# A decoder layer with attention, retention and routed experts on one core: first stage reordered, norm factor on ACT, transposes that accumulate

## The chip, the cores and the metric

The program runs on one core of a Trainium2 chip. Its time is device microseconds: the median of three runs is 1015.34 us (1014.36 to 1017.56).

## The reference

x and ctx have 128 sequences of 64 tokens of 128 dimensions, float32. Three blocks follow each other, each with its residual and a layer norm without weights.

```python
def layernorm(x): return (x - mean(x)) / sqrt(var(x) + 1e-5)

def reference(x, ctx, Wq, Wk, Wv, Wo, bo, gate, w1, w2, w3):
    # 1. self-attention, 16 heads of 8
    q, k, v = (heads(t @ W.T) for t, W in ((x, Wq), (x, Wk), (x, Wv)))
    att = softmax(q @ k.T / sqrt(8))
    x = layernorm(x + merge(att @ v) @ Wo.T + bo)
    # 2. retention: scores with a decay mask, no softmax
    q, k, v = xpos(heads(x)), xpos(heads(ctx), downscale=True), heads(ctx)
    x = layernorm(x + merge((q @ k.T * decay) @ v))
    # 3. two of eight experts per token, inner size 512
    w, e = top_k(x @ gate, 2); w = softmax(w)
    y = sum(w[i] * ((silu(x @ w1[e[i]]) * (x @ w3[e[i]])) @ w2[e[i]]) for i in (0, 1))
    return layernorm(x + y)
```

The shape in the first block is unusual: `x` has 128 sequences, and attention runs among the 64 tokens of each.

## The kernel before

It has three stages. The **first stage** takes 32 pairs of tiles (a tile is 128 tokens, two sequences) through both attention blocks, computes the gate, and scatters each token's row twice (once for each chosen expert) to DRAM (`xs`, "routed_rows"). The **second stage** gathers 71 tiles of 256 routed rows of one expert each, runs the expert, and scatters the results to "token_halves". The **third stage** adds the two halves of a token and norms.

All engines run the first stage in lockstep of a kind, without a common clock. `run_steps` (L178) writes out, for each engine, its steps in a row; in step s a function that stands at `at(lag)` works on item s - lag. Since `A_FIRST` is 32, all of the first stage is written out, without a loop. The order of an engine's work is the order of the `at` calls in its own `step` function, by hand: L457 on SyncE, L715 on PE, L975 on ACT, L1331 on DVE, L1571 on POOL. Each function first waits on semaphores (`wait`, `wait_ring`, `wait_last`) and counts up one of its own. Where PSUM is shared between engines, `wait_last` (L150) names, of several events, the one that comes last in that order.

An item's way: SyncE loads x (L461). PE transposes it (`tokens_across`, L532), ACT copies it to `x_t` (L858), PE projects q, k, v (L540), ACT copies q and v (L865). DVE forms all products of q and k (`products`, L1145), PE sums them over dimensions (`scores`, L556), DVE and PE find the maximum over all keys (L1155 to L1174, L567 to L577), DVE subtracts it, ACT takes the exponential (L873). POOL multiplies by v (`weighted`, L1545, eight instructions), PE sums over keys (`sums`, L579), DVE divides (L1182, L1189). SyncE stores the heads to DRAM, waits for that store, and reloads them in transposed order (L468 to L481). PE adds projection, bias and x (`residual`, L593). Then the first norm: DVE has statistics (`spread`, `moments`), then `variances` (L1224) for the first norm of one item and the second norm of an earlier one together (`NORM_GAP` = 2), POOL raises to the power -0.5 and forms the shift (L1523, L1534), ACT applies them (`first_norm`, L898). PE transposes keys and queries, as sums of two products with the identity (L610, L619). Retention scores, mask, values and head selection follow (L639, L1235, L649, L663), the second residual and norm (L1242, L944), the gate and the top two with their ranks (L675 to L703, L1252 to L1329), and POOL's indirect scatters (`scatter`, L1559). ACT's second norm writes into a ring of four, so it waits for the scatters of the item four before it (L948).

Three weight matrices are loaded in float32 and split into a high and a low half-precision part during the first steps, on DVE and ACT (L1108 to L1143, L835); their loads stand at the head of ACT's queue (L829). `stand` (L404) writes a marker and counts a semaphore; it occurs in all three stages.

The lines that the prediction's steps touch:

```python
wait_ring(it, routed_out, RING, 64)                    # second_norm, L948
wait(it, marked[n], 1)                                 # stand, L407
wait(it, nb_ready)                                     # first_norm, L901
eng.matmul(XKT[:, P * u:P * u + P], xk_a[:, u, :], ident, start=True, stop=False)   # keys_across, L615
```

## Time and profile before

| | |
|---|---|
| median of 3 runs | 1015.34 us |
| profiled execution, its span from first to last instruction | 1027.0 us |
| PE busy | 839.8 us (82%), 12164 instructions |
| DVE busy | 794.7 us (77%), 2219 |
| POOL busy | 654.8 us (64%), 738 |
| ACT busy | 607.7 us (59%), 1416 |
| DMA | 72.7 MB, mean 71 GB/s |

The time of the profiled execution is known by its span alone; it is 1.1% above the median of the timed runs. In the profile, PE is the matrix engine and PEld its weight loads, DVE the vector engine, ACT the scalar engine, POOL the general one and SP the engine that only issues transfers. A row of a group of instructions gives the line, engine, operation, what is written and read with its shape, how many; then the busy time in us and the mean duration of one in ns; then the idle time of the engine just before them and what ended it. The means of one instruction hold its whole way through the engine, so instructions that follow each other overlap. A granted clock of 1.00 is 2.4 GHz on PE, 0.50 is 1.2 GHz, and a number in between is a mix over the stretch.

### The profile page before, as it was taken

Reading aid. Unit: us, or ns where it says so; the run is one execution under the profiler, and the core shown is the slowest. Engines: PE = TensorE matmul, PEld = TensorE weight load, DVE = VectorE, ACT = ScalarE, POOL = GpSimd, SP = SyncE. Lnnn points to the kernel's source line nnn. Section 1 sums busy time; section 2 is a strip of 40 time slices with the busy share of each in tenths; the row PEclk is TensorE's granted clock in tenths of the full one; section 3 lists DMA queues with packets and bytes.
Section 4 is the critical chain, followed back from the end, with each engine's and each line's share of the span. In section 5 each row is a group of like instructions: output and inputs, shape, how many; then the busy total and the mean of one; then the engine's idle time right before and its main releaser. Section 6 shows DMA issues by size and latency. Waiting matters only on the chain.

```text
span 1027.0 us, 35115 instructions
## 1 busy us (share of the span) xinstructions
PE 839.8 (82%) x12164; PEld 639.6 (62%) x12164; DVE 794.7 (77%) x2219; ACT 607.7 (59%) x1416; POOL 654.8 (64%) x738
## 2 busy tenths in 40 slices
PE   1667699999999999989979770699999999999600
PEld 1445466666666666656655440599899999999500
DVE  4787899998988989878856642588888888888575
ACT  1123457667667777666766851466666666666355
POOL 0338776699989999988997456044444444444443
PEclk9687899999999999999998965799999999999855
DMA  9312122122232231212222002222222222222186
GB/s 307 79 27 48 35 52 54 36 66 67 47 72 52 65 68 50 65 37 60 47 50 63 23 22 63 66 64 61 61 63 65 65 62 64 63 61 59 45 257 222
DMA packets 145303, 72.72 MB, mean 71 GB/s; under 512 B 75024, under 2 KB 134544, under 8 KB 145136
## 3 DMA queue, kind: packets, MB, share of 16 engines
q1 hardware_dynamic: 124800, 40.56, 17.1%
q0 software_dynamic: 8640, 17.84, 5.2%
q10 hardware_dynamic: 11696, 12.08, 3.6%
q8 instruction: 105, 1.72, 0.7%
q14 instruction: 62, 0.51, 0.2%
HBM read 42.11 MB, written 28.34 MB: 69 GB/s over the span
## 4 chain that ended last, share of the span: by engine, by line
PE 33%; POOL 28%; issue 11%; DVE 3%; DMA 2%; another core or an unknown queue 1%; ACT 1%; POOLq 0%; SPq 0%; DVEq 0%; ACTq 0%
POOL prod_ev L1551 14%; POOL routed_rows L1568 9%; PE QKV L773 9%; PE ST L773 9%; PE XT L801 5%; PE SC L801 5%; POOL rs L1531 3%; DMA prod_ev<-token_halves 1%; DMA routed_rows<-xe,pos 1%; PE YY L589 1%; POOL frs L1613 1%; PE YY L791 1%; PE TR L791 1%; PE SC L562 1%
## 5 line engine op out<-in xcount | busy, mean ns | idle before, releaser
L1551 POOL TENSOR_TENSOR prod_ev<-e_sb,q_v 128x512 f32<-128x512 f32 x256 | 300.3, 1206 | 77.5 <-PE YY L589 40.1
L1600 POOL DMA_INDIRECT token_halves<-w_new,tok_i x142 | 137.9, 971 | 32.5 <-issue 22.2
L1568 POOL DMA_INDIRECT routed_rows<-xe,pos x128 | 131.2, 1025 | 30.4 <-issue 30.0
L1151 DVE TENSOR_TENSOR prod_qk<-q_v,QKV 128x2048 f32<-128x2048 f32 x64 | 145.4, 2274 | 4.9 <-ACT q_v L870 4.9
L1453 DVE TENSOR_TENSOR prod_ev<-prod_qk,prod_ev 128x1024 f16<-128x1024 f32 x71 | 87.0, 1225 | 56.1 <-ACT prod_ev L1028 31.1
L773 PE MATMUL QKV<-k_t,w_hl 128*128 128x256 f16 x852 | 117.2, 274 | 0.0
L773 PE MATMUL ST<-k_t,w_hl 128*128 128x256 f16 x852 | 116.9, 274 | 0.0
L411 POOL TENSOR_TENSOR marks<-half_c 128x1 f32<-128x1 f32 x103 | 19.7, 192 | 149.7 <-DVE w_new L1469 149.1
L1037 ACT ACTIVATE prod_qk<-QKV,silu_scale 128x512 f32<-128x512 f32 x142 | 90.0, 683 | 41.3 <-PE QKV L773 41.3
L1028 ACT CAST prod_ev<-prod_qk 128x1024 f16<-128x1024 f32 x71 | 74.2, 1045 | 62.9 <-DVE prod_qk L1479 62.9
L1479 DVE SCALAR_TENSOR_TENSOR prod_qk<-ST,hid_scale,prod_qk 128x512 f32<-128x512 f32 x142 | 99.5, 742 | 2.9 <-PE ST L773 1.8
L924 ACT ACTIVATE q<-XT,tab 128x256 f32<-128x256 f32 x256 | 96.6, 495 | 0.0
L589 PE MATMUL YY<-prod_ev,tab 128*32 128x144 f32 x2048 | 83.3, 304 | 11.4 <-DVE m_two L1167 7.2
L951 ACT ACTIVATE xe<-res,nb,rs 128x128 f32<-128x128 f32 x128 | 52.7, 483 | 64.3 <-DMA routed_rows<-xe,pos 64.3
L773 PEld LDWEIGHTS ST<-k_t,w_hl 128*128 x852 | 83.7, 98 | 10.0
L1239 DVE TENSOR_TENSOR sm<-ST,tab 128x1024 f32<-128x1024 f32 x64 | 77.7, 1215 | 15.2 <-PE ST L643 12.9
L773 PEld LDWEIGHTS QKV<-k_t,w_hl 128*128 x852 | 80.9, 98 | 9.0 <-issue 0.4
L643 PE MATMUL ST<-q,k_t 64*64 64x512 f32 x512 | 74.2, 651 | 8.1 <-ACT q L924 5.4
L589 PEld LDWEIGHTS YY<-prod_ev,tab 128*32 128x32 f32 x2048 | 62.3, 115 | 24.7 <-issue 23.2
L562 PE MATMUL SC<-prod_qk,tab 128*32 128x256 f32 x1024 | 68.0, 408 | 10.7 <-ACT e_sb L878 6.8
L1531 POOL TENSOR_TENSOR rs<-ve,half_c 128x4 f32<-128x4 f32 x34 | 37.8, 1113 | 45.6 <-DVE ve L1233 44.4
L801 PE MATMUL XT<-w_hl,prod_ev 128*128 x864 | 61.2, 223 | 3.1 <-DVE prod_ev L1453 3.1
(171 smaller groups left out, 1785.9 us busy)
## 6 DMA issues: line engine op xcount, KB each, us to landing
w_new<-routed_rows SPq DMA_DIRECT2D x71, 130.0 KB
prod_ev<-token_halves SPq DMA_DIRECT2D x16, 512.0 KB, 4.9
x_sb<-x SPq DMA_DIRECT2D x32, 128.0 KB, 2.8
x_res<-x SPq DMA_DIRECT2D x128, 32.0 KB
head_rows<-o_n SPq DMA_DIRECT2D x32, 128.0 KB
o_t<-head_rows SPq DMA_DIRECT2D x64, 64.0 KB
ctx_sb<-ctx SPq DMA_DIRECT2D x32, 128.0 KB
out<-prod_qk ACTq DMA_DIRECT2D x16, 256.0 KB, 4.0
```

The lines of the kernel that those rows point to most:

```text
L562: mm = eng.matmul(SC[QUARTER * g:QUARTER * g + QUARTER, 256 * u:256 * u + 256].rearrange("p (q i j) -> p q i j", q=4, j=4), pick, prod_qk[ ...
L589: mm = eng.matmul(SUMS[QUARTER * q:QUARTER * q + QUARTER, u, :], pick, prod_ev[:, u, q, j, :, :].rearrange("p i d -> p (i d)"), start=(j = ...
L773: mm = eng.matmul(out[:, 512 * half + TILE * n:512 * half + TILE * (n + 1)], w_hl[:, wp, bass.ds(no * inner + P * (2 * half + n), P)], x_h ...
L801: mm = eng.matmul(YB[down.slot(2)][:, P * u:P * u + P], h[:, down.slot(2), TILE * n + P * u:TILE * n + P * u + P], w2_hl[:, wp, cols], sta ...
L924: ins = eng.activation(q8[:, it.slot(2), :, :, r, :].rearrange("p b u t -> p (b u) t"), QT.rearrange("p (n t) -> p n t", t=S), ACT.Copy, s ...
L1037: eng.activation(sil[:, t.slot(2), 512 * half:512 * half + 512], QKV[:, 512 * half:512 * half + 512], ACT.Silu, scale=silu_scale[:, :]).th ...
L1151: eng.tensor_tensor(prod_qk[:, u, :, :].rearrange("p d (i j) -> p d i j", j=NH), q.unsqueeze(3).to_broadcast([P, HD, NH, NH]), k.unsqueeze ...
L1453: eng.tensor_tensor(hid_lo[:, t.slot(2), :], hid[:, t.slot(2), :], hid_hi[:, t.slot(2), :], ALU.subtract).then_inc(hlo_ready, 1)
L1479: eng.scalar_tensor_tensor(out=hid[:, t.slot(2), cols], in0=ST[:, cols], scalar=hid_scale[:, :], in1=sil[:, t.slot(2), cols], op0=ALU.mult ...
L1551: ins = eng.tensor_tensor(prod_ev[:, u, q, :, :, 0:HD], e_sb[:, it.slot(2), u, 64 * q:64 * q + 64].rearrange("p (i j) -> p j i", j=4).unsq ...
L1568: eng.indirect_dma_start(out=xs, out_offset=bass.IndirectOffsetOnAxis(ap=pos[:, r, 2 * u + k:2 * u + k + 1], axis=0), in_=xe[:, r, u, k, : ...
L1600: eng.indirect_dma_start(out=halves, out_offset=bass.IndirectOffsetOnAxis(ap=tok_i[:, s, u:u + 1], axis=0), in_=yw[:, s, u, :], in_offset= ...
```

## The change

- Every engine's order and lags in the first stage are new. On PE, an item's `tokens_across` moves from lag 0 to 2 and `ranks` from 13 to 14; on DVE, score maxima from 3 to 5 and positions from 14 to 15; on POOL, the products from 0 and 1 to 6 and 7, the scatters from 11 to 16 (first half) and 17 (second half). The waits of `wait_last` follow.
- The norm factor: POOL's power and shift and DVE's `variances` go. ACT takes a logarithm of the variance plus epsilon and an exponential of minus half of it, for each norm by itself; DVE forms the shift.
- Transposes of keys and queries are marked as transposes and accumulate in PSUM. The residual's x comes from the stored transpose `x_t` (a ring of eight now) by an accumulating transpose; the separate load `x_res` goes. x is loaded in row order, by four requests.
- SyncE: x of the first item directly behind the identity; the heads are stored by four requests and reloaded a step later, without the store being waited for at once; two of the three weights are requested by SyncE behind the fourth x, one by ACT after the first x has landed.
- The two one-hot operations are one; the markers go in all stages; the third stage's steps are all written out (`C_FIRST` from 8 to 16).

```diff
-    PE_LAGS, ACT_LAGS, DVE_LAGS, POOL_LAGS, SP_LAGS = 13, 13, 14, 11, 9
+    PE_LAGS, ACT_LAGS, DVE_LAGS, POOL_LAGS, SP_LAGS = 14, 15, 15, 17, 10
-    C_FIRST, C_LAGS = 8, 3
+    C_FIRST, C_LAGS = n_chunks_c, 3
-        x_t = sb("x_t", [2, 2, P])
+        x_t = sb("x_t", [X_RING, 2, P])                 # X_RING = 8
...
         def _(eng):                                     # SyncE
+            def load_x(it):
+                wait(it, xt_done, RING)
+                for u in range(2):
+                    for b in range(2):
+                        eng.dma_start(x_sb[S * u:S * u + S, it.slot(RING), b, :], x_rows[it.number()][u][b]
+                                      ).then_inc(x_in[it.slot(RING)], 16)
+            def store_heads(it):
+                wait(it, on_ready)
+                wait(it, y_done, RING)
+                for u in range(2):
+                    for b in range(2):
+                        eng.dma_start(head_rows[it.slot(RING)][u][b],
+                                      o_n[S * u:S * u + S, it.slot(2), b, :, :].rearrange("p d h -> p (d h)")
+                                      ).then_inc(heads_out[it.slot(RING)], 16)
+            def load_heads(it):
+                r = it.slot(RING)
+                wait_ring(it, heads_out, per=64)
+                for u in range(2):
+                    eng.dma_start(o_t[:, r, u, :, :],
+                                  heads[r, u].rearrange("(g t) (d h) -> (t d) g h", t=NH, d=HD)).then_inc(y_in[r], 16)
+            eng.dma_start(tab[:, 0:split], table[:, 0:split]).then_inc(ident_in, 16)
+            load_x(Item(eng, None, None, 0))
+            eng.dma_start(w_qkv_sb[:, :], w_qkv).then_inc(qkv_in, 16)
+            eng.dma_start(tab[:, split:], table[:, split:]).then_inc(tab_in, 16)
...
             def step(at):
+                if it := at(9):
+                    store_heads(it)
+                if it := at(9):
+                    load_context(it)
+                if (it := at(0)) and it.off > 0:
+                    load_x(it)
+                    if it.off == 3:
+                        load_weights(2)
+                        load_weights(1)
+                if it := at(10):
+                    load_heads(it)
...
             def residual(it):                           # PE
-                wait_ring(it, y_in, per=96)
+                wait_ring(it, y_in, per=32)
-                eng.matmul(Y, ones_bf[:, :], bo_bf[:, :], start=True, stop=False, skip_group_check=True)
                 for b in range(2):
+                    eng.matmul(Y[:, P * b:P * b + P], x_t[:, it.slot(X_RING), b, :], ident,
+                               is_transpose=True, start=(b == 0), stop=False, skip_group_check=True)
+                eng.matmul(Y, ones_bf[:, :], bo_bf[:, :], start=False, stop=False, skip_group_check=True)
...
-                    mm = eng.matmul(Y[:, P * b:P * b + P], ident, x_res[:, it.slot(RING), b, :], start=False, stop=True,
-                                    skip_group_check=True)
...
-                    eng.matmul(XKT[:, P * u:P * u + P], xk_a[:, u, :], ident, start=True, stop=False)
-                    mm = eng.matmul(XKT[:, P * u:P * u + P], xk_b[:, u, :], ident, start=False, stop=True)
+                    eng.matmul(XKT[:, P * u:P * u + P], xk_a[:, u, :], ident, is_transpose=True, start=True, stop=False)
+                    mm = eng.matmul(XKT[:, P * u:P * u + P], xk_b[:, u, :], ident, is_transpose=True, start=False, stop=True)
...
             def step(at):                               # PE, new order: function(lag)
+                # half_over(5) rows_across(13) ret_values(12) residual(9) quarter_over(5) own_heads(12)
+                # project(3) gates(13) tokens_across(2) ret_scores(11, 0) scores(4, 0) ranks(14) sums(6, 0)
+                # ret_scores(11, 1) keys_across(10) scores(4, 1) queries_across(10) sums(6, 1) spread_max
...
+            eng.wait_ge(x_in[0], 64)                    # ACT
+            eng.dma_start(fresh(0).rearrange("p (e i) -> p e i", e=n_exp), w1.rearrange("e h i -> h e i")).then_inc(w_in[0], 16)
...
             def tokens_across(it):
                 wait(it, xt_done)
-                wait(it, qkv_done, 2)
+                wait(it, y_done, X_RING)
...
+            def logarithm(it, norm):
+                s = it.slot(2)
+                wait(it, (mv1_ready, mv2_ready)[norm])
+                wait(it, rs_ready[norm], 2)
+                eng.activation(lnv[:, s, norm, :], mv[:, s, norm, :, 1], ACT.Ln, bias=eps_c[:, 0:1]).then_inc(ln_ready[norm], 1)
+            def one_over_std(it, norm):
+                s = it.slot(2)
+                wait(it, ln_ready[norm])
+                wait(it, nb_ready[norm], 2)
+                wait(it, (x1_ready, x2_ready)[norm], 2)
+                eng.activation(rs[:, s, norm, :], lnv[:, s, norm, :], ACT.Exp, scale=-0.5).then_inc(rs_ready[norm], 1)
...
             def step(at):                               # ACT, new order: function(lag)
+                # beside(6, 0) row_ids(15) queries_across(11) ret_across(12) logarithm(10, 0) one_over_std(10, 0)
+                # keys_across(11) rows_across(13) blocks(11) other_over_own(14) exponent(5) logarithm(12, 1)
+                # residual(9) project(3) tokens_across(2) one_over_std(12, 1) first_norm(10) beside(6, 1) second_norm(12)
...
-            def variances(c, d):                        # DVE
+            def norm_shift(it, norm):
+                s = it.slot(2)
+                wait(it, rs_ready[norm])
+                wait(it, (x1_ready, x2_ready)[norm], 2)
+                eng.scalar_tensor_tensor(out=nb[:, s, norm, :], in0=mv[:, s, norm, :, 0], scalar=-1.0, in1=rs[:, s, norm, :],
+                                         op0=ALU.mult, op1=ALU.mult).then_inc(nb_ready[norm], 1)
...
             def step(at):                               # DVE, new order: function(lag)
+                # gate_weights(15) mask(12, 1) top_places(14) score_max(5) products(4, 0) max_of_two(5) products(4, 1)
+                # max_of_four(5) one_over(7) counts(15) subtract_max(5) chosen_places(15) one_hot(14) positions(15)
+                # second_residual(12) norm_shift(10, 0) spread(12) moments(12) divide(7) chosen(14) keys_by_cos(10)
+                # mask(11, 0) keys_by_sin(10) norm_shift(12, 1) queries_by_cos(10) queries_by_sin(10) places(14)
+                # logits(13) spread(9) moments(9) top_values(13)
+                # and in steps 4 to 9: measure, weight_scale, low_part, blank_pad
...
             def step(at):                               # POOL, new order: function(lag)
+                # weighted(7, 1, 1) scatter(17, 1) scatter(16, 0) weighted(6, 0, 0) weighted(6, 0, 1) weighted(6, 1, 0)
```

## Rows read from the trace of the kernel before

**Rows 1.** Busy time by stretch: length, engines (instructions), clock, DMA share, GB/s.

```profile
core 0: us, PE busy (x) PEld busy (x) DVE busy (x) ACT busy (x) POOL busy (x), PEclk, DMA share, GB/s
0.00:128.97 128.97, 74.51 (x1201) 51.22 (x1205) 93.34 (x111) 35.29 (x55) 61.77 (x56) 0.83 0.37 99
128.97:512.28 383.31, 366.30 (x6439) 249.61 (x6435) 342.75 (x1013) 263.54 (x719) 333.88 (x339) 1.00 0.25 56
512.28:641.00 128.72, 84.67 (x979) 54.84 (x978) 65.32 (x337) 74.56 (x222) 86.04 (x100) 0.79 0.17 45
641.00:971.00 330.00, 314.34 (x3550) 283.93 (x3550) 261.33 (x584) 207.93 (x356) 150.42 (x213) 0.97 0.22 61
971.00:1027.00 56.00, 0.00 (x0) 0.00 (x0) 31.98 (x176) 26.34 (x64) 22.66 (x33) 0.50 0.72 227
```

**Rows 2.** First and last start of score maxima, positions and scatters, by line.

```profile
L1161 DVE TENSOR_REDUCE m_own<-SC x32: 674/692/693, 30.4 to 512.3; 128x128 f32<-128x512 f32 x32
L1328 DVE TENSOR_REDUCE pos<-posw x32: 170/179/186, 189.3 to 630.2; 128x4 int32<-128x32 f32 x32
L1568 POOL DMA_INDIRECT routed_rows<-xe,pos x128: 954/983/1277, 202.3 to 637.6; - x128
```

**Rows 3.** Busy time by stretch: one full step, one of the drain, its end.

```profile
318.51:334.37 15.86, 15.41 (x274) 10.67 (x272) 14.23 (x47) 11.15 (x32) 14.80 (x16) 1.00 0.30 64
566.43:577.54 11.11, 9.38 (x104) 5.89 (x103) 7.06 (x37) 8.84 (x27) 5.71 (x7) 1.00 0.08 26
590.00:616.00 26.00, 18.37 (x168) 11.09 (x168) 13.16 (x76) 15.10 (x48) 12.76 (x17) 0.65 0.07 21
```

**Rows 4.** POOL's instructions by line in one step's length (333.52 to 349.38).

```profile
L1551 POOL TENSOR_TENSOR prod_ev<-e_sb,q_v 128x512 f32<-128x512 f32 x8 | 9.1, 1168 | 0.0
L1568 POOL DMA_INDIRECT routed_rows<-xe,pos x4 | 4.1, 1034 | 0.9 <-issue 0.9
L1531 POOL TENSOR_TENSOR rs<-ve,half_c 128x4 f32<-128x4 f32 x2 | 2.1, 1046 | 0.0
L1542 POOL TENSOR_TENSOR nb<-nm,rs 128x4 f32<-128x4 f32 x1 | 0.2, 202 | 0.1
L411 POOL TENSOR_TENSOR marks<-half_c 128x1 f32<-128x1 f32 x1 | 0.2, 183 | 0.0
```

**Rows 5.** ACT's longest wait from 200 to 520 us: total, times, longest.

```profile
ACT xe L951 <- DMA routed_rows<-xe,pos: 46.1, 17, 4.0
```

**Rows 6.** PE's x products and transposes by line, same step as Rows 4.

```profile
L606 PE MATMUL TR<-x_res,tab 128*128 128x128 f32 x4 | 1.0, 326 | 0.0
L624 PE MATMUL XT<-tab,xq_a 128*128 128x128 f32 x4 | 0.9, 295 | 0.0
L537 PE MATMUL XT<-tab,x_sb 128*128 128x128 f32 x2 | 0.4, 300 | 0.0
```

**Rows 7.** Small ACT activations and all table loads by line, whole span.

```profile
L969 ACT ACTIVATE ex<-mx 128x1 f32<-128x1 f32 x128 | 27.3, 289 | 0.2 <-DVE mx L1266 0.2
L863 ACT ACT_TABLE_LOAD x1 | 1.3, 1283 | 17.9 <-issue 17.9
L1037 ACT ACT_TABLE_LOAD x1 | 1.3, 1283 | 0.0
```

**Rows 8.** ACT in order of time around the second load: start, length, instruction.

```profile
652.56 0.41 ACT L1033 ACTIVATE w_new<-w_new 128x256 f32<-128x256 f32 x1
652.98 1.28 ACT L1037 ACT_TABLE_LOAD   x1
654.28 0.69 ACT L1037 ACTIVATE prod_qk<-QKV,silu_scale 128x512 f32<-128x512 f32 x1
```

**Rows 9.** The start in order of time, ACT and its queue, DVE.

```profile
1.24 14.69 ACTq L826 DMA_DIRECT2D w_hl<-w  x4
...
19.16 0.37 ACT L863 COPY x_t<-XT 128x256 f32<-128x256 f32 x1
...
23.74 4.48 DVE L1151 TENSOR_TENSOR prod_qk<-q_v,QKV 128x2048 f32<-128x2048 f32 x2 [4.87 <-ACT q_v L870]
```

**Rows 10.** The last second norm on ACT, in order of time.

```profile
619.34 1.65 ACT L951 ACTIVATE xe<-res,nb,rs 128x128 f32<-128x128 f32 x4 [6.62 <-DMA routed_rows<-xe,pos]
```

More of the change, by code:

```diff
@@ L399, in build @@
             sem(n) for n in ("fsum_ready", "fstat_ready", "fmv_ready", "fve_ready", "frs_ready", "fout_ready"))
-        marks = sb("marks", [7])
-        marked = [sem(f"marked{n}") for n in range(7)]
-        def stand(it, n):
-            wait(it, marked[n], 1)
-            if n not in (4, 5):
-                it.eng.memset(marks[:, n:n + 1], 0.0).then_inc(marked[n], 1)
-            else:
-                it.eng.tensor_tensor(marks[:, n:n + 1], half_c[:, 0:1], half_c[:, 0:1], ALU.add).then_inc(marked[n], 1)
         def fresh(n):
@@ L729, in step @@
+            def step(at):
+                if it := at(5):
+                    half_over(it)
+                if it := at(13):
+                    rows_across(it)
+                if it := at(12):
+                    ret_values(it)
+                if it := at(9):
+                    residual(it)
                 if it := at(5):
-                    sums(it, 0)
-                if it := at(3):
                     quarter_over(it)
                 if it := at(12):
+                    own_heads(it)
+                if it := at(3):
+                    project(it)
+                if it := at(13):
@@ new lines, in step @@
+                if it := at(14):
+                    ranks(it)
+                if it := at(6):
+                    sums(it, 0)
+                if it := at(11):
+                    ret_scores(it, 1)
+                if it := at(10):
+                    keys_across(it)
+                if it := at(4):
+                    scores(it, 1)
+                if it := at(10):
+                    queries_across(it)
+                if it := at(6):
+                    sums(it, 1)
+                if at_step(at, 4):
+                    spread_max(0)
@@ new lines, in step @@
+                if it := at(11):
+                    queries_across(it)
+                if it := at(12):
+                    ret_across(it)
+                if it := at(10):
+                    logarithm(it, 0)
+                if it := at(10):
+                    one_over_std(it, 0)
+                if it := at(11):
+                    keys_across(it)
+                if it := at(13):
+                    rows_across(it)
+                if it := at(11):
+                    blocks(it)
+                if it := at(14):
+                    other_over_own(it)
@@ L985, in step @@
+                if it := at(5):
+                    exponent(it)
+                if it := at(12):
+                    logarithm(it, 1)
+                if it := at(9):
+                    residual(it)
+                if it := at(3):
+                    project(it)
+                if it := at(2):
+                    tokens_across(it)
+                if it := at(12):
+                    one_over_std(it, 1)
+                if it := at(10):
                     first_norm(it)
-                if it := at(4):
-                    beside(it, 0)
@@ L1002, in step @@
-                if it := at(8):
-                    queries_across(it)
-                if it := at(6):
-                    residual(it)
-                weights(at)
+                    second_norm(it)
+                if at_step(at, 4):
+                    high_part(0)
+                if at_step(at, 7):
+                    high_part(1)
+                if at_step(at, 8):
+                    high_part(2)
             run_steps(eng, n_duo, A_FIRST, ACT_LAGS, step)
@@ new lines, in step @@
+                if it := at(5):
+                    max_of_two(it)
+                if it := at(4):
+                    products(it, 1)
+                if it := at(5):
+                    max_of_four(it)
+                if it := at(7):
+                    one_over(it)
+                if it := at(15):
+                    counts(it)
+                if it := at(5):
+                    subtract_max(it)
+                if it := at(15):
+                    chosen_places(it)
+                if it := at(14):
+                    one_hot(it)
@@ new lines, in step @@
+                if it := at(15):
+                    positions(it)
+                if it := at(12):
+                    second_residual(it)
+                if it := at(10):
+                    norm_shift(it, 0)
+                if it := at(12):
+                    spread(it, res2, stat2, res2_ready, stat2_ready, mv2_ready)
+                if it := at(12):
+                    moments(it, 1, stat2, stat2_ready, mv2_ready)
+                if it := at(7):
+                    divide(it)
+                if it := at(14):
+                    chosen(it)
```

495 lines of the change are left out of this document (191 added, 304 removed).

## The prediction

> **What bounds the kernel now.** I read the table of stages first [rows 1]. The first stage (thirty-two pairs of 128-token tiles) takes 641 of the 1027.0 us of the profiled execution; the expert stage after it has PE busy 314 of 330 us, and the last one waits for transfers (DMA share 0.72, PE idle). The change leaves those two alone but for marker instructions and one loop written out. So the question is what a step of the first stage costs. I cut the table where the eighth of the 32 score maxima starts, at 128.97 us, and where the last does, at 512.3 [rows 2]: 24 steps in 383.3 us, 15.97 us each.
>
> In the windows of single steps [rows 3] the reader is to see who fills one: PE 15.41 of 15.86 us, POOL 14.80, DVE 14.23, ACT 11.15. POOL's idle time is 0.9 us in front of its scatters, and it ends by "issue": nothing outside POOL shortens it [rows 4]. So PE and POOL both bound the step, DVE is 1.6 us behind, and ACT has 4.7 us to spare. Much of ACT's spare time is forced: it waited 46.1 us of 320 for scatters of four items back [rows 5]. In the drain, when POOL has no products left, a step takes 11.1 us with ACT busy 8.84 [rows 3].
>
> The timed median is 1015.34 us, 1.1% under the span. I add up in the span, and scale the difference by 0.989 onto the median.
>
> **POOL.** Removed per step: the power (1.05), the shift (0.20) and a mark (0.18) [rows 4], 1.4 us. Left are eight products (9.1), four scatters (4.1) and their issue time (0.9): 14.2 us or slightly more.
>
> **PE.** A product with the identity is two instructions (L606 has 4 per step for two), a transpose is one (L537 has 2 for two) [rows 6]. Adding x by transposing its stored transpose replaces four instructions of 1.0 us together by two of about 0.4: 0.6 saved. The key and query sums have four such terms of four instructions (L624 is one, 0.9 us); each term becomes two transposes of 0.4, so 2.0 us go if nothing overlaps. Neighbours do overlap here (the step's groups add up to more than its length), so I take half. PE falls by about 1.6 us, to some 14. That accumulation costs a transpose nothing has no row; I bound it between that and the price of the old products (gain 0), and take the gain.
>
> **DVE.** It loses two small operations of the joint variance step, four marks and one of two one-hot operations, and gains two shift operations. Each of these is between 0.06 and 0.4 us and they nearly cancel; moments now follow the statistics directly, which can expose about 0.1 us twice. I keep 14.2, plus or minus 0.4.
>
> **SyncE.** x is now requested in four pieces and the separate row copy goes; the heads are stored in four pieces instead of one, and the reload moves one step later, behind the next item's store, the context and the x request. The queue no longer stands still for the store to land. Requests per step go from nine to eleven at about half a microsecond each, 5 to 6 us of a 16 us step: hidden. If that cover were gone, the residual sum on PE would wait, and with it the second half of the maximum behind it.
>
> **Added waits.** The copy of x's transpose waits for the residual of eight items before; that is one step earlier in PE's order and costs nothing. The second norm of item i+4 (ACT step i+16) still waits for the scatters of item i, whose second half now stands in POOL's step i+17. POOL must therefore run ahead of ACT by about half a step. It has products that the sums need only late, so it can; if not, ACT stands before its last operation, and PE's next transposes behind it.
>
> **ACT, the part that decides.** Four small activations per step come to ACT: a logarithm and an exponential for each of the two norms. The nearest row is L969 at 289 ns, overlapped to 0.21 [rows 7]; I take 0.25, so 1.0 us, and ACT is at 12.15. The open cost is the function table. The trace has two table loads of 1283 ns [rows 7]: one before the first copy, under which every copy, scaled pass and Exp of the first stage runs, and one directly ahead of the first Silu. Around that second load nothing overlaps: the operation before it ends at 652.97, the load stands from 652.98 to 654.26, the Silu starts at 654.28 [rows 8]. No row shows a logarithm. The low end is no load at all, if the table in use also serves it. The high end follows from the new order on ACT: log, exp, then the exponentials of gate and scores, then log, copies, exp. Each change between the functions would be a load, four per step. I take the high end, because its row is the nearest: a function new to the stage brought a load in front of itself, and nothing in the kernel names a table that serves both. Four loads are 5.13 us, and the lost overlap of neighbours (about 0.1 each) adds 0.4: ACT 12.15 + 5.5 = 17.7 us of work per step. That is more than PE, POOL or DVE need, so ACT becomes the bound, in order and with little idle time, and what POOL and PE save is cover.
>
> The Trainium skill ("ScalarE: Activation LUTs", What ACT_TABLE_LOAD costs) gives 1283 ns for the load, as the trace has, and about 1380 ns of drain beside it. Rows 8 show no such drain. With it the step would be an estimated 23 us and the kernel near 1175 us.
>
> **The sum.** Start: before, the first copy of x's transpose waited until 19.16 us, because ACT first issued 14.69 us of weight requests, and the first score products began at 23.74 [rows 9]. Now x comes before the weights and ACT issues one of them; about 6 us earlier. But one weight maximum (4.4 us on DVE, which ran in that gap) moves into the filled steps. Net -3 us (between -12 and +5). Middle: three steps at about 16.6 (not all ACT work is in yet) and 21 at 17.7 make 421.5 against 383.3: +38. End: from the last score maximum to the last scatter's landing the old trace has 128.7 us. Now two steps at 17.7 and 16.4, four at 15.3 (8.84 + 1.0 + 5.5), then 11 and 8, make 114; from the last second norm (619.3 to 621.0 [rows 10]) to the last positions (630.2 [rows 2]) 9.4 more, four scatters 5.3 and the landing 2: 131, +2 us. There is one step fewer between maximum and positions; the loads eat it. Last stage: the loop written out, -1. Together +36: 1063 us of span, 1015.3 + 36 = 1051 us timed.
>
> **Rivals.**
> (1) One table for both functions. The trace cannot exclude it, as it has no logarithm. Then ACT is at 12.15, and POOL (14.2) and DVE (14.2) bound at about 14.7 with some waits: 24 x 14.7 = 353, -30; the drain's steps fall to about 10, with one fewer, 102 against 128.7, -26; start -3, last stage -1. Sum -60 of span, 956 us: faster. The point from which it decides is fewer than about two loads per step (11.15 + 1.0 + 2.8 = 15, under the old step). The Trainium skill ("ScalarE: Activation LUTs", Table sets: the hidden batching unit) speaks for it: a set with both exp and ln exists, and ln followed by exp costs one load.
> (2) Loads, and a slower PE on top. PE would work 14 of 17.7 us, 79%. Two stretches of the drain lie on either side: 566 to 578 with PE busy 9.38 of 11.11 us at clock 1.00, and 590 to 616 with 18.37 of 26 at 0.65 [rows 3]; the start, at 74.5 of 129, has 0.83 [rows 1]. At 0.83 PE's 14 us become some 17.5, as long as ACT's work, and the two wait for each other: about 1.2 us per step, 24 steps, 1080 us.
> (3) The edits do little: loads hide in ACT's 4.7 us of waiting and the rest is eaten by POOL and DVE. ACT's sum speaks against it (17.7 is 1.8 over the old step). About 1015 us.
>
> **Chances.** The forecast 0.62, (2) 0.15, (1) 0.17, (3) 0.03, a dearer load 0.03. Likeliest 1051, its own range 1030 to 1075. For eight in ten I leave out (1) and the dearest loads: 1010 to 1095. A change under about 0.3% cannot be told from none; so faster 0.17, within 0.03, slower 0.80.
>
> **What will show it.** Table loads on ACT: about 128 instead of one in the first stage (right) or none (then rival 1). ACT busy near 17 of 17.7 us per step, POOL 14 to 14.5 with idle time that ends by PE, and no power on POOL. PE's key and query sums at half the instruction count. If steps take 17.7 us while ACT is idle for over 2 us of them, my step on ACT is wrong and a wait (the scatter's landing, rival 2's clock) is what binds.

## The result and the profile after

The changed kernel takes 1110.6 us (median of four runs, 1109.7 to 1112.4) against 1016.0 for the kernel before in the same runs: 1.091 times as long, 95% interval 1.087 to 1.095. It is slower, as forecast, but by 94.6 us where I had 36, and outside the range that I gave.

The table of stretches of the changed kernel, cut at the same events as [rows 1] (eighth score maximum, last score maximum, last scatter, end of the expert stage; columns as there):

```profile
0.00:119.55 119.55, 74.94 (x1301) 52.83 (x1302) 96.06 (x114) 45.46 (x69) 62.92 (x60) 0.81 0.37 102
119.55:597.41 477.86, 380.62 (x6170) 241.35 (x6169) 383.63 (x912) 408.88 (x924) 304.75 (x277) 0.87 0.18 39
597.41:729.00 131.59, 78.82 (x825) 45.03 (x825) 67.84 (x286) 109.10 (x261) 57.91 (x58) 0.69 0.19 42
729.00:1057.00 328.00, 314.28 (x3550) 283.56 (x3550) 255.38 (x568) 214.84 (x356) 135.89 (x142) 0.97 0.21 60
1057.00:1110.50 53.50, 0.00 (x0) 0.00 (x0) 31.40 (x160) 26.34 (x64) 21.09 (x32) 0.50 0.73 236
```

Against [rows 1]: the start is 9.4 us shorter (I had 3), the 24 steps of the middle 94.6 longer (I had 38), the drain 2.9 longer (I had 2), the two stages after it together 4.5 shorter (I had 1). That makes 83.5 us of span. The timed difference is 11 us larger because the profiled execution of the kernel before ran 1.1% above its median and that of the changed kernel did not. In the span, then, the whole miss is in the middle: 19.91 us per step instead of 17.56.

The score maxima (least, median and most ns, first and last start) answer the first line of [rows 2]; the new table loads, by line over the whole span (busy time, mean ns, idle time before), answer [rows 7]:

```profile
L1180 DVE TENSOR_REDUCE m_own<-SC x32: 669/671/1089, 29.0 to 597.4; 128x128 f32<-128x512 f32 x32
```

```profile
L895 ACT ACT_TABLE_LOAD x64 | 82.1, 1283 | 1.1
L903 ACT ACT_TABLE_LOAD x64 | 82.1, 1283 | 1.1
```

There are 128 loads more than the two of [rows 7], each 1283 ns and none with a drain beside it: 164 us of ACT. Next, single steps (same columns as the stretches), against the first of [rows 3]. Fifteen of the 24 take 20.55 to 20.58 us like the first line; four in a row take 19.2 to 19.7 like the second, and five at the ends take 17.7 to 19.2:

```profile
437.69:458.27 20.58, 16.55 (x259) 10.54 (x259) 16.20 (x41) 17.13 (x41) 13.07 (x12) 0.83 0.18 40
338.47:357.65 19.18, 14.45 (x251) 9.35 (x255) 16.07 (x40) 17.11 (x40) 12.77 (x12) 0.93 0.20 43
```

ACT's work is 17.1 us, near the 17.7 that I had added up; but ACT is idle 3.4 us of the step, and idle time above 2 us is the sign that I had named for a wrong step on ACT. The waits of ACT in the first of these steps (total, times, longest), then the values' product on PE in the first and in the second step (count, busy time, mean ns):

```profile
ACT rt L949 <- PE ST L667: 2.0, 1, 2.0
ACT xe L846 <- DVE xe L1311: 1.2, 1, 1.2
```

```profile
L667 PE MATMUL ST<-sm,ctx_bd 128*32 128x128 f32 x32 | 1.9, 421 | 0.0
L667 PE MATMUL ST<-sm,ctx_bd 128*32 128x128 f32 x32 | 1.1, 276 | 0.0
```

The clock of these two products (columns as in the stretches), and what PE waited for four microseconds before the first of them, in the order of time:

```profile
439.57:441.51 1.94, 1.94 (x34) 1.46 (x34) 1.94 (x3) 0.00 (x0) 1.94 (x3) 0.50 0.00 0
339.83:340.91 1.08, 1.08 (x34) 0.88 (x34) 1.08 (x1) 0.48 (x2) 1.08 (x2) 1.00 0.07 15
```

```profile
435.40 0.33 PE L636 MATMUL XT<-tab,xq_a 128*128 128x128 f32 x1 [2.62 <-DVE xq_b L1240]
```

The first product runs at the lower level of the clock (0.50), the second at the upper one. Both waits are at the head of ACT's step. ACT waits for the gate weights (DVE) and then for the values' product, which PE does on the mask that DVE makes right behind the gate weights. What DVE did before that stands in the order of time in the same step, ACT first (start, length, instruction, idle time before it), then POOL (its four products together, and the last three of them singly) and DVE:

```profile
442.17 1.28 ACT L895 ACT_TABLE_LOAD   x1
443.47 0.30 ACT L895 ACTIVATE lnv<-mv,eps_c 128x2 f32<-128x2 f32 x1
443.78 1.28 ACT L903 ACT_TABLE_LOAD   x1
...
450.86 1.28 ACT L903 ACT_TABLE_LOAD   x1
452.26 0.86 ACT L912 ACTIVATE x<-res,nb,rs 128x128 f32<-128x128 f32 x2
```

```profile
450.92 4.72 POOL L1560 TENSOR_TENSOR prod_ev<-e_sb,q_v 128x512 f32<-128x512 f32 x4 [2.94 <-PE YY L599]
452.04 1.17 POOL L1560 TENSOR_TENSOR prod_ev<-e_sb,q_v 128x512 f32<-128x512 f32 x1
453.18 1.16 POOL L1560 TENSOR_TENSOR prod_ev<-e_sb,q_v 128x512 f32<-128x512 f32 x1
454.30 1.34 POOL L1560 TENSOR_TENSOR prod_ev<-e_sb,q_v 128x512 f32<-128x512 f32 x1
...
445.82 0.15 DVE L1248 SCALAR_TENSOR_TENSOR nb<-mv,rs 128x2 f32<-128x2 f32 x1
...
452.39 0.84 DVE L1248 SCALAR_TENSOR_TENSOR nb<-mv,rs 128x2 f32<-128x2 f32 x1 [2.95 <-ACT rs L903]
453.16 1.46 DVE L1234 TENSOR_TENSOR xq_a<-x,tab 128x256 f32<-128x256 f32 x1
454.54 1.38 DVE L1240 TENSOR_TENSOR xq_b<-x,tab 128x256 f32<-128x256 f32 x1
```

DVE stands 2.95 us until the fourth load is over. Then the shift takes 0.84 us where the same line takes 0.15 earlier in the step, and the two query products 1.46 and 1.38 where the key products, of the same shape, take 0.41: just while POOL does four products in a row, each 1.18 us. Each of the three ends just behind a POOL product: at 453.23, 454.62 and 455.92, where the products end at 453.21, 454.34 and 455.64. In the kernel before the query products fell mostly beside POOL's scatters and took 0.41:

```profile
336.75 1.21 POOL L1568 DMA_INDIRECT routed_rows<-xe,pos  x1 [0.17 <-issue]
336.62 0.41 DVE L1215 TENSOR_TENSOR xq_a<-x,tab 128x256 f32<-128x256 f32 x1
```

So the ring is: ACT (load, exponential, first norm), DVE (three slow operations, gate weights, mask), PE (values), ACT.

POOL's rows in that step answer [rows 4]: 13.1 us of work, no power.

```profile
L1560 POOL TENSOR_TENSOR prod_ev<-e_sb,q_v 128x512 f32<-128x512 f32 x8 | 9.2, 1183 | 5.5 <-PE YY L599 5.5
L1576 POOL DMA_INDIRECT routed_rows<-xe,pos x4 | 3.9, 970 | 1.9 <-DVE pos L1340 1.2 <-issue 0.6
```

### The profile page after: what moved, and what is told of

Same layout as the page of the kernel before. It is cut to its first block, busy times and chain, and to the rows that moved or that the text cites. A ratio compares the mean times of both kernels' runs of the same rounds, so it can differ in the third digit from the quotient of the medians.

```text
span 1110.5 us, 34400 instructions
## 1 busy us (share of the span) xinstructions
PE 848.7 (76%) x11844; PEld 622.8 (56%) x11844; DVE 834.3 (75%) x2039; ACT 804.6 (72%) x1672; POOL 582.6 (52%) x567
## 4 chain that ended last, share of the span: by engine, by line
PE 39%; ACT 24%; issue 16%; DVE 10%; POOL 3%; DMA 1%; ACTq 1%; DVEq 1%; SPq 0%; POOLq 0%
PE QKV L780 8%; PE ST L780 8%; ACT L895 7%; PE XT L808 5%; PE SC L808 5%; PE ST L667 4%; ACT L903 3%; DVE xq_b L1240 3%; ACT ex L976 2%; ACT x L912 2%; ACT ctx_bd L941 2%; ACT q L931 2%; PE YY L581 2%; POOL frs L1614 1%; PE ST L652 1%
## 5 line engine op out<-in xcount | busy, mean ns | idle before, releaser
L1576 POOL DMA_INDIRECT routed_rows<-xe,pos x128 | 124.0, 969 | 102.9 <-DVE pos L1340 70.4
L1059 ACT ACTIVATE prod_qk<-QKV,silu_scale 128x512 f32<-128x512 f32 x142 | 96.2, 678 | 12.2 <-PE QKV L780 9.3
L1248 DVE SCALAR_TENSOR_TENSOR nb<-mv,rs 128x2 f32<-128x2 f32 x64 | 28.4, 444 | 87.2 <-ACT rs L903 87.1
L599 PE MATMUL YY<-prod_ev,tab 128*32 128x144 f32 x2048 | 90.0, 325 | 0.0
L652 PE MATMUL ST<-q,k_t 64*64 64x512 f32 x512 | 81.8, 714 | 5.7 <-DVE sm L1255 5.7
L895 ACT ACT_TABLE_LOAD x64 | 82.1, 1283 | 1.1
L903 ACT ACT_TABLE_LOAD x64 | 82.1, 1283 | 1.1
L572 PE MATMUL SC<-prod_qk,tab 128*32 128x256 f32 x1024 | 71.4, 399 | 12.1 <-ACT e_sb L870 12.1
L558 PE MATMUL QKV<-w_qkv_sb,x_t 128*32 128x96 f32 x2048 | 59.0, 277 | 21.5 <-DVE prod_qk L1170 14.5
L599 PEld LDWEIGHTS YY<-prod_ev,tab 128*32 128x32 f32 x2048 | 65.7, 121 | 10.4 <-issue 5.7
```

The lines of the kernel that those rows point to most:

```text
L599: mm = eng.matmul(SUMS[QUARTER * q:QUARTER * q + QUARTER, u, :], pick, prod_ev[:, u, q, j, :, :].rearrange("p i d -> p (i d)"), start=(j = ...
L895: eng.activation(lnv[:, s, norm, :], mv[:, s, norm, :, 1], ACT.Ln, bias=eps_c[:, 0:1]).then_inc(ln_ready[norm], 1)
L903: eng.activation(rs[:, s, norm, :], lnv[:, s, norm, :], ACT.Exp, scale=-0.5).then_inc(rs_ready[norm], 1)
L1059: eng.activation(sil[:, t.slot(2), 512 * half:512 * half + 512], QKV[:, 512 * half:512 * half + 512], ACT.Silu, scale=silu_scale[:, :]).th ...
L1576: eng.indirect_dma_start(out=xs, out_offset=bass.IndirectOffsetOnAxis(ap=pos[:, r, 2 * u + k:2 * u + k + 1], axis=0), in_=xe[:, r, u, k, : ...
```

## The experiments

All are edits of the changed kernel, unless the kernel before is named. "Step" is the middle (eighth to last score maximum) over 24; the usual step stands in brackets.

| kernel | loads per step | step, us | time, us | ratio to before (95%) |
|---|---|---|---|---|
| changed | 4 | 19.91 (20.57) | 1110.6 | 1.087 to 1.095 |
| one_table | 0 | 14.29 (14.30) | 947.7 | 0.928 to 0.937 |
| two_loads | 2 | 17.28 (17.48) | 1044.3 | 1.023 to 1.030 |
| half_products | 4 | 17.77 (17.87) | 1060.1 | 1.040 to 1.047 |
| half_2loads | 2 | 16.55 (16.64) | 1026.8 | 1.006 to 1.013 |
| half_1table | 0 | 15.34 | 979.5 | 0.957 to 0.967 |
| busy_pe | 4 | 19.03 (19.21) | 1105.3 | 1.083 to 1.090 |
| mask_early | 4 | 18.64 (18.15, 19.45) | 1093.6 | 1.073 to 1.080 |
| mask_early_1table | 0 | 16.45 (16.49) | 1015.9 | 0.997 to 1.002 |
| products_1table | 0 | 14.85 (14.93) | 969.4 | 0.950 to 0.956 |
| pool_waits | 4 | 29.53 (30.55) | 1408.1 | 1.379 to 1.388 |
| before_log (order of before) | 2 | 16.94 | 1060.7 | 1.030 to 1.046 |
| before_log_1table (order of before) | 0 | 15.35 | 999.8 | 0.981 to 0.987 |

**The loads taken out (one_table).**

```diff
 def _(eng):   # ScalarE
+    eng.preload_act_table_set("natural_log_exp_and_others")
     eng.wait_ge(x_in[0], 64)
```

> The changed kernel with one instruction more: ahead of everything ScalarE loads the table set that serves both the logarithm and the exponential. Nothing else is altered. The 128 table loads of 1283 ns then go. Theory (the loads lie on a ring of waits ACT, DVE, PE, ACT, so each counts in full): 128 x 1.283 = 164 us less than 1110.6, 946 us, and a step of 20.56 - 5.13 = 15.4 us. Forecast's own rival 1 (POOL and DVE bound at 14.7): 956 us. Rival (the new order costs time by itself and the loads hide in its waits): above 1016, the time before.

Measured: 947.7 us. The loads by line, and a step:

```profile
L825 ACT ACT_TABLE_LOAD x1 | 1.3, 1283 | 0.7 <-PEq L1644 0.7
L1060 ACT ACT_TABLE_LOAD x1 | 1.3, 1283 | 0.0
```

```profile
403.60:417.90 14.30, 13.72 (x264) 8.83 (x267) 13.57 (x40) 11.87 (x35) 13.06 (x13) 1.00 0.23 49
```

Two loads are left of 130, and 163 us are gone, as much as the loads' own busy time. The usual step fell by more than its four loads (6.27 instead of 5.13), the middle as a whole by 135 us, and the start hardly at all (the eighth maximum is at 118.8 instead of 119.55). PE is now busy 96% of a step, the clock is full, and DVE's query products take 0.42 us. The theory's 946 us came true by luck in part: the middle gives 135 us where four full loads in each of 24 steps make 123, and the rest 28 where the other eight steps make 41. The new order with one table is 6.8% faster than the kernel before. It is the best version of the study.

**Half of the loads (two_loads).**

```diff
-    logarithm(at 10, 0); one_over_std(at 10, 0)    # ScalarE, after ret_across
     logarithm(at 12, 1)
+    logarithm(at 10, 0)
...
     one_over_std(at 12, 1)
+    one_over_std(at 10, 0)
# VectorE: norm_shift(at 10, 0) from behind second_residual to ahead of norm_shift(at 12, 1)
```

> The changed kernel with the two logarithms side by side on ScalarE and the two exponentials of the norms side by side, and the first norm's shift on VectorE behind the second statistics: two loads per step instead of four, same work otherwise. Theory (loads count in full): 64 fewer x 1.283 = 82 us, 1028 us, less what the first norm now waits for the shift (up to 1 us per step, 24 us): 1028 to 1055. Rival (only a part of the loads is on the path, the rest is the blocked VectorE): above 1065.

Measured: 1044.3 us, in the theory's interval, step 17.48. ACT works 14.7 us of it. Two loads out took 3.1 us off the usual step, and taking out the other two 3.2: again over 1.5 us for a load of 1.28. The first 3.1 hold the clock too: these steps run at a granted 1.00, and busy_pe, below, has the four loads at that clock and takes 19.21, so 1.36 of the 3.1 are the clock's, and 1.73 go to the two loads and the moved shift together.

**POOL made to wait (pool_waits).**

```diff
 def step(at):   # POOL
+    if it := at(10):
+        wait(it, xqb_ready)
     if it := at(6):
         weighted(it, 0, 0)
```

> The changed kernel, loads and all, but POOL begins the products of a step only when VectorE has finished the two rotary query products (one more wait on POOL). In the changed kernel the norm shift and these two take 0.84, 1.46 and 1.38 us while POOL's products run, and 0.15, 0.41 and 0.41 us elsewhere. Theory (VectorE is held until the running POOL product ends, and this is on the ring of waits): 2.7 us off every step, 17.9 instead of 20.56, and 1110.6 - 24 x 2.7 = about 1045 us. Rival (ACT's idle 2.8 us come from a longer ring in which POOL plays no part): the three take 1.0 us, the time is saved nowhere, a step stays at 20.5 and the kernel at 1105 to 1115. Rival 2 (POOL's products are late next): slower than 1115.

Measured: 1408.1 us, rival 2, and far beyond what I thought it could cost. DVE's lines over two steps (count, busy, mean ns, idle before), then the waits of that stretch:

```profile
L1234 DVE TENSOR_TENSOR xq_a<-x,tab 128x256 f32<-128x256 f32 x2 | 0.9, 426 | 1.2 <-ACT x L912 1.2
L1240 DVE TENSOR_TENSOR xq_b<-x,tab 128x256 f32<-128x256 f32 x2 | 0.8, 420 | 0.0
L1248 DVE SCALAR_TENSOR_TENSOR nb<-mv,rs 128x2 f32<-128x2 f32 x4 | 0.6, 160 | 7.3 <-ACT rs L903 7.3
```

```profile
POOL prod_ev L1560 <- DVE xq_b L1240: 33.0, 2, 16.5
ACT xe L958 <- DMA routed_rows<-xe,pos: 26.5, 2, 13.3
```

The first half of the theory holds: with POOL idle the three operations take 0.16, 0.43 and 0.42 us. But POOL now stands 16.5 us per step, its scatters come late, and ACT's second norm waits 13.3 us for the scatters of four items before. That is the wait of which the prediction said that POOL must run ahead of ACT. This run can't tell what the blocked DVE costs.

**POOL's products in halves (half_products).**

```diff
 for q in range(2 * half, 2 * half + 2):
-    product of quarter q (128x512)
+    for j in range(0, 4, 2):
+        product of rows j, j + 1 of quarter q (128x256)
```

> The changed kernel, four table loads per step and all, with each of POOL's 8 products of a step (1.15 us) cut into two of half the size, in the same place, with the same waits. Theory (a VectorE operation with two inputs in SBUF waits until the running POOL operation ends, and that wait is on the ring): the norm shift, 0.84 us in the changed kernel, and the two query products, 1.46 and 1.38, wait at most half as long and come to about 0.5, 0.9 and 0.9; 1.2 to 1.4 us off every step, 19.2 instead of 20.56, the kernel near 1080 us. Rival (the three are slow but not on the ring; ACT's waits have another cause): the three are shorter, the step stays at 20.5, 1105 to 1115 us. Rival 2 (POOL's 10% more work counts): slower than 1115.

Measured: 1060.1 us, 50 less, more than expected. A step, and DVE's lines in it:

```profile
426.10:443.98 17.88, 13.93 (x259) 8.91 (x259) 14.47 (x40) 17.04 (x41) 14.46 (x21) 1.00 0.22 47
```

```profile
L1240 DVE TENSOR_TENSOR xq_b<-x,tab 128x256 f32<-128x256 f32 x1 | 0.9, 894 | 0.0
L1248 DVE SCALAR_TENSOR_TENSOR nb<-mv,rs 128x2 f32<-128x2 f32 x2 | 0.6, 318 | 2.9 <-ACT rs L903 2.9
L1234 DVE TENSOR_TENSOR xq_a<-x,tab 128x256 f32<-128x256 f32 x1 | 0.6, 616 | 0.3 <-ACT x L912 0.3
```

The three operations together go from 3.68 to about 2.0 us (the shift's mean is over both norms; the other one takes 0.15). POOL does more work, ACT the same, and ACT is now busy 17.04 of 17.88 us: this is the step that I had forecast, 17.7. By the Trainium skill ("SBUF — State Buffer", SBUF: two separate sides) a DVE operation with two inputs in SBUF and a POOL operation that reads SBUF take turns on a shared port, each for a whole instruction. The trace agrees: POOL operations of half the size hold these three for 1.0 us above their undisturbed 0.97 instead of 2.7, and the mask, which has one input in PSUM, took 1.21 us beside POOL's products and 1.22 beside its scatters in the kernel before.

**The other two with halves (half_2loads, half_1table).** The same cut on top of two_loads and of one_table.

> Two loads per step (as in two_loads) and POOL's products cut in halves (as in half_products). There ACT was busy 17.0 of 17.87 us of a step, here 17.0 - 2.57 = 14.45, and the first norm waits for the shift (1.07 us per step in two_loads). Theory (with the blocked VectorE eased, ACT's own work is the floor and nothing else): 15.3 to 15.9 us per step, 1060 - 24 x 2.2 - 8 = about 1000 us. Rival (a load is dearer than its 1.28 us because of a ring that has its own length): 16.5 or more, 1025 us or more.

> POOL's products cut in halves, with the one table set and no loads in the steps. In the kernel with one table nothing but 0.2 us per step of VectorE was blocked. Theory (halves help only where VectorE is blocked on the path; POOL's work rises from 13.1 to 14.5 us per step and so becomes the bound): 14.6 to 15.0 us per step, 955 to 970 us, slower than the one table alone at 948. Rival (halves help by themselves, because the sums on PE can start earlier or VectorE is freer): 945 us or less.

Measured: 1026.8 us, the rival's figure, and 979.5, the theory's direction but 10 us beyond its interval. A step of the first, and the line of the places in the second over 220 us:

```profile
375.30:391.90 16.60, 13.86 (x259) 8.84 (x259) 14.43 (x40) 14.60 (x38) 14.39 (x21) 1.00 0.23 51
```

```profile
L1333 DVE TENSOR_TENSOR posw<-oh,posf 128x32 f32<-128x32 f32 x14 | 17.1, 1224 | 0.0
```

With two loads no engine is at its own work: four of them have 13.9 to 14.6 us and wait for each other for 2 (ACT 0.6 for the values, 0.6 for the first shift, 0.5 for DVE's subtraction, 0.3 for PE's residual). The floor by ACT's work holds with four loads only; from half_2loads to half_products 64 loads cost 33 us, 0.5 each. In the second another DVE operation, the places, is held: 1.22 us in the mean, where one_table has 0.36 in the same stretch, and up to 2.12 in the whole kernel. That is as long as three POOL products, which take 0.66 now, so an operation of DVE can be held past the one that runs when it comes. one_table has the plainest case, behind its last score maximum, where the places are held until the last of seven whole products ends, at 482.52:

```profile
475.47 7.11 DVE L1333 TENSOR_TENSOR posw<-oh,posf 128x32 f32<-128x32 f32 x1
474.63 7.89 POOL L1561 TENSOR_TENSOR prod_ev<-e_sb,q_v 128x512 f32<-128x512 f32 x7
```

Halves are no gain by themselves.

**PE kept busy (busy_pe).**

```diff
 def queries_across(it):   # PE
+    wait_last(it, n_duo, ...)
+    for n in range(20):
+        eng.transpose(QT[:, P * (n % 2):P * (n % 2) + P], const("half_over"), ident)
     wait(it, xqb_ready)
-    wait_last(it, n_duo, ...)
```

> The changed kernel, loads and POOL as they are, with useless work for PE: 20 transposes of a constant table per step, into the place that the query transposes overwrite next, in the 2.6 us in which PE stands idle until VectorE has the second query product. In the changed kernel most steps (20.57 us) run at a granted clock of 0.83 and take ACT 2.0 us of waiting for the values' product (421 ns a piece); a few run at 0.93 to 0.95, take 19.2 us, and ACT waits 0.6 us (276 ns a piece). Theory (the idle PE loses its clock and pays for it in the ring): granted clock at or above 0.95, all steps at 19.2 or less, 24 x 1.2 = 30 us less: 1075 to 1090 us, with more work done. Rival (the clock is no part of it; the filler only delays the query transposes): 1110 us or more.

Measured: step and clock as the theory has them, the total not (1105.3). A step, and ACT's wait for the values in it:

```profile
390.60:409.90 19.30, 16.26 (x279) 11.08 (x279) 16.18 (x41) 17.27 (x41) 13.22 (x13) 1.00 0.19 43
```

```profile
ACT rt L951 <- PE ST L669: 0.7, 1, 0.7
```

With useless work the clock stays at the upper level in these steps, each of them takes 19.2 us instead of 20.57, and the wait for the values falls from 2.0 to 0.7. The middle is 21 us shorter (456.6 instead of 477.9). But 3.4 us more go in the start and 12 after the last maximum. There the filler may only delay; no run separates it.

**The mask earlier on DVE (mask_early, and with one table).**

```diff
-gate_weights(at 15); mask(at 12, 1)      # VectorE, first in the step
...
+gate_weights(at 14); mask(at 11, 1)
 norm_shift(at 12, 1)
```

> The changed kernel with all its loads and POOL as it is; on VectorE alone the second mask of a step and the gate weights move from the start of the next step to ahead of the second norm's shift, where VectorE stood idle for 3.0 us waiting for the exponential. ACT's two waits of a step (for the gate weights 1.2 us, for the values' product on PE behind the mask 1.7) then no longer stand behind the blocked query products. Theory (ACT's own 17.4 us of work are the floor, and the 2.8 us above it come from the blocked VectorE on the way back to ACT): a step of 17.5 to 18.2 us, 1040 to 1060 us. Rival (each load counts 1.55 us in the ring whatever VectorE does, as 14.3, 17.48 and 20.56 us for none, two and four loads suggest): a step above 19.5, over 1085 us.

> The same move on VectorE, with the one table set loaded at the start, so with no load in the steps. In the kernel with one table PE was busy 13.74 of 14.27 us of a step, DVE 13.6, POOL 13.0, ACT 11.9. Theory (three engines near their own work, ACT no bound): little to win, 14.0 to 14.3 us per step, 940 to 950 us. Rival (VectorE reaches the mask too early, waits for PE's scores there and holds the query products): 14.6 or more, 955 to 975 us.

Measured: 1093.6 us, on the rival's side (over 1085) though its mean step, 18.64, lies between the two; and 1015.9, beyond the rival. DVE's wait in the first (total, times, longest), and the second's second query product, both over 220 us:

```profile
DVE sm L1255 <- PE ST L652: 28.2, 22, 2.3
```

```profile
L1241 DVE TENSOR_TENSOR xq_b<-x,tab 128x256 f32<-128x256 f32 x13 | 17.9, 1378 | 0.0
```

DVE comes to the masks before PE has the scores, 2.4 us per step. In the first, steps of 18.15 us at a granted clock of 0.98 to 1.00 take turns with steps of 19.4 at 0.92 to 0.93: the theory's step holds for the former, and the clock parts the two. The query products stay blocked in the first, and one of them becomes blocked in the second, where it was free. The same kernel without loads is 68 us slower by this: in this order it matters which DVE operation meets POOL's products.

**The transposes undone (products_1table).** one_table without the transpose form in the sums of x, keys and queries.

```diff
-eng.matmul(QT[...], xq_a[:, b, :], ident, is_transpose=True, start=True, stop=False)
+eng.matmul(QT[...], xq_a[:, b, :], ident, start=True, stop=False)
```

> One table set, with the accumulating transposes of x, of the keys and of the queries turned back into products with the identity (same instructions, without the transpose form; the rest of the changed order stays). It prices the transposes. With them PE is busy 13.74 of 14.27 us of a step. Theory (PE is the bound now, and a product with the identity is two passes instead of one: 2.6 us of PE per step by the prediction's sum, of which half overlaps): 15.4 to 15.9 us per step, 32 x 1.3 = 42 us more, 980 to 1000 us. Rival (accumulation made the transposes as dear as products, or PE has room): 945 to 955 us.

Measured: 969.4 us; the direction, at half the price. A step:

```profile
403.70:418.60 14.90, 14.90 (x270) 10.15 (x270) 13.76 (x39) 11.78 (x35) 13.12 (x13) 1.00 0.22 47
```

PE has no gap left. The accumulating transposes save it 1.2 us per step (14.90 to 13.72), and 0.6 of that reaches the step.

**The norm factor alone, in the order of before (before_log, before_log_1table).**

```diff
-# POOL: rs = ve ** -0.5
+# ScalarE, after row_ids: lnv = Ln(ve); rs = Exp(-0.5 * lnv)
```

> The kernel before, in its old order, with the norm factor alone moved from POOL's power to ScalarE (one logarithm and one exponential of 128x4 per step, for both norms), the shift still on POOL. Two table loads per step come with it: ACT 11.15 + 0.5 + 2.57 = 14.2 us of work in a step of 15.9. Theory (loads cost where ACT has no room or stands in a ring of waits; here ACT has 4.7 us): the step stays near 15.9 or gains some of POOL's 1.05, 1005 to 1030 us. Rival (the loads lie between variance and first norm, and the whole ring waits for them here too): 1.3 to 2.6 us per step, 1050 to 1080 us.

> The kernel before in its old order, the norm factor alone on ScalarE (as in the run before_log), with the one table set loaded at the start: no loads. It tells what the move of the norm factor is worth without the new order. Theory (POOL and PE both bound the old step of 15.75; POOL loses 1.05 but PE keeps 15.4): 15.4 to 15.7 us per step, 1000 to 1015 us, so that most of the 68 us that the changed kernel gains with one table come from the order and PE's shorter sums. Rival (POOL's power was what set the old step): 14.7 us per step, 975 to 990 us.

Measured: 1060.7 (the rival) and 999.8 us (the theory). Two steps of the first, and waits in the former of them:

```profile
264.20:284.50 20.30, 18.33 (x273) 11.87 (x275) 14.98 (x44) 15.55 (x38) 13.34 (x14) 0.83 0.27 58
284.50:300.50 16.00, 15.15 (x273) 10.41 (x273) 14.37 (x44) 12.77 (x34) 13.54 (x14) 1.00 0.15 44
```

```profile
POOL nb L1550 <- ACT rs L911: 4.7, 1, 4.7
ACT xe L967 <- DMA routed_rows<-xe,pos: 2.6, 1, 2.6
```

64 loads cost 61 us in a place where ACT had 4.7 us of every step to spare: 0.95 us each. The long step is also the one with the low clock, and no run separates the two here. POOL waits for the factor, its scatters come late, and ACT waits for these. Without loads, the factor on ACT is worth 16 us in the old order; the other 52 of the 68 that one_table gains over the kernel before come with the rest of the change.

## Why the prediction was wrong

**Right.** That each switch between logarithm and exponential is a load, four per step and 128 in all; that nothing in the kernel gives a table for both, so that rival 1 does not come by itself; that no drain comes beside a load; ACT's work (17.7 forecast, 17.1 busy and some 0.2 between instructions); POOL without the power (14.2 forecast with its issue time, 13.1 busy and 0.6 of issue); the drain (131 forecast, 131.6); that a transpose can be accumulated at its own price (PE forecast at some 14, in one_table 13.7). The Trainium skill's table sets ("ScalarE: Activation LUTs", Table sets: the hidden batching unit), by which logarithm and exponential share one load, hold only where that set is asked for, as one_table shows; left alone the changed kernel loads 128 times. Rival 1's price, 956 us, was near: 947.7, with a step of 14.29 where I had 14.7.

**The step that failed** is "so ACT becomes the bound, in order and with little idle time, and what POOL and PE save is cover". ACT is not a queue that the others feed in good time. It stands in a ring with DVE and PE, and the forecast took DVE's durations from rows in which they were undisturbed: 14.2 us per step, where DVE came to 16.2. Per step:

- Forecast 17.56. With POOL's products in halves the kernel does 17.77, with ACT busy 95%.
- Blocked DVE: from 17.77 to 19.03 (half_products to busy_pe, both at the upper clock), 1.26 us, 30 us in 24 steps. The shift and the two query products meet POOL's products.
- Clock: from 19.03 to 19.91 (busy_pe to the changed kernel), 0.88 us, 21 us. While DVE is late PE stands idle, 2.6 us for the second query product, and the step's granted clock goes to 0.83, a mean between its two levels (1.2 and 2.4 GHz). The values' product, four microseconds later, runs at the lower level and is slower by half, and ACT waits for it.

That is 51 of the 56 us that the middle is off. The split is by kernels that differ in one thing each from the changed one; the two halves are not independent, as with the blocked DVE eased the clock is back too (half_products, 1.00).

**The rivals.** Rival 2 (loads and a slower clock, 1080) named the second half, but for another reason: I had PE's own work reach ACT's, while the clock acts through one short product in the ring (and its sum was off: 14 us at 0.83 are 16.9, not 17.5). Rival 3 (loads hide in ACT's spare time) is refuted even for the old order, by before_log. No rival had the blocked DVE, though the kernel before has a case of it. Its one-hot operations, with two inputs in SBUF, take 0.17 us at the median and 1.20 at most (ns, least, median and most); the long ones ran beside POOL's products, as at 304 us, where a pair of them took 1.21 beside a product of 1.22:

```profile
L1284 DVE TENSOR_TENSOR oh<-tab,ix x64: 139/167/1200, 175.3 to 625.1; 128x16 f32<-128x16 f32 x64
```

**Sizes.** The start was mis-sized: the first copy on ACT is at 12.75 us instead of 19.16 [rows 9], the 6 us that I had, but the 3 that I gave back for a weight maximum in the filled steps did not come, and the eighth maximum is 9.4 earlier.

Open: why two loads with halves still take 16.6 us per step where no engine has over 14.6 of work. The waits are spread over four places, and no run separates them.

## What to carry to other kernels

An instruction that adds 1.3 us to an engine in a ring of waits can cost anything from a part of its length to more than it. Per load of 1.28 us the kernel's time grew by 0.5 (half_2loads to half_products), 0.95 (before_log) or 1.5 us (one_table to two_loads), and the engine's idle share did not tell which. Look for the ring (who waits for this engine, and for whom does it wait) before calling idle time cover. If two functions alternate on ScalarE, ask for the set that has both, and count the loads in the trace. When the order of a step shifts, check which VectorE operations with two SBUF inputs now fall beside POOL's products, and read their durations there, not where they ran before.

## What the runs showed of the hardware

POOL's products of 1.18 us held VectorE operations with two inputs in SBUF: 0.15 us became 0.84, 0.41 became 1.46 and 1.38, and each ended within 0.3 us of the end of a product; with POOL operations of half the size, 0.49, 0.62 and 0.89; with POOL idle, 0.16, 0.43 and 0.42. In a row of products one operation can be held past several: 7.11 us in one_table, where the same line takes 0.18 undisturbed. What decides how long, no run here shows. Useless work on an idle TensorE made a step faster: 20 transposes more per step, granted clock 1.00 instead of 0.83, step 19.2 instead of 20.57 us.
